# A window-attention block on one NeuronCore: x2 evicted by ScalarE, other orders on all queues, and groups handed to the second convolution from SBUF to SBUF

## The reference

```python
x = x + _conv_bn(x, dw0_w, dw0_s, dw0_b, groups=C)       # 3x3 depthwise
x = x + _ffn(x, f0_w1, f0_s1, f0_b1, f0_w2, f0_s2, f0_b2) # 64 -> 128 -> relu -> 64
x = x + _windowed_attn(x, wq, wkv, pos, scale_p, dwc_w, dwc_b, proj_w, proj_b)
x = x + _conv_bn(x, dw1_w, dw1_s, dw1_b, groups=C)
x = x + _ffn(x, f1_w1, f1_s1, f1_b1, f1_w2, f1_s2, f1_b2)
```

## Time and profile before

| | us |
|---|---|
| median of 3 runs (194.59 to 196.1) | 194.67 |
| the profiled execution, its own time | 195.5 |
| its span, first to last instruction | 193.7 |

### The profile page before, as it was taken

One profiled execution on the slowest core, in us unless ns is written; L12 is line 12 of the kernel. 1 busy time (PEld: TensorE's weight loads), 2 busy tenths in 40 slices (PEclk: granted clock), 3 DMA queues, 4 the chain that ended last, 5 costly groups with the idle time before them and its releaser, 6 DMA issues.

```text
span 193.7 us, 6645 instructions
## 1 busy us (share of the span) xinstructions
PE 164.9 (85%) x2840; PEld 79.9 (41%) x2840; DVE 109.2 (56%) x269; ACT 78.7 (41%) x144; POOL 67.7 (35%) x99
## 2 busy tenths in 40 slices
PE   7977989369929959989999476999997999995994
PEld 3322432334514525736636255358343434321141
DVE  1185269924664668769869869679254256002044
ACT  2052558224334326365480450672351615441122
POOL 3000207035145152254375384392046336330000
PEclk9999999856997999999999997899999999997599
DMA  5999998500000000000005306217017174757813
GB/s 150 284 292 229 208 216 167 141 3 0 3 2 3 0 3 3 3 3 5 3 3 157 58 3 170 43 58 154 8 61 175 63 167 130 174 170 187 210 54 108
DMA packets 18028, 18.77 MB, mean 97 GB/s; under 512 B 1104, under 2 KB 17744, under 8 KB 17872
## 3 DMA queue, kind: packets, MB, share of 16 engines
q1 hardware_dynamic: 17568, 17.83, 38.6%
q10 hardware_dynamic: 432, 0.52, 1.1%
HBM read 14.16 MB, written 4.19 MB: 95 GB/s over the span
## 4 chain that ended last, share of the span: by engine, by line
PE 37%; issue 13%; DVE 11%; POOL 9%; ACT 5%; DMA 4%; SPq 1%; DVEq 0%; POOLq 0%; ACTq 0%
PE ps L623 9%; PE ps L703 4%; PE ps L649 3%; PE ps L643 3%; PE ps L688 3%; POOL y L372 3%; DMA mid<-x 2%; DMA xc<-mid 2%; PE ps L824 2%; POOL x L382 2%; PE ps L815 2%; PE ps L727 2%; DVE k L997 2%; PE ps L763 2%; POOL k L349 2%
## 5 line engine op out<-in xcount | busy, mean ns | idle before, releaser
L623 PE MATMUL ps<-xc,dwf 96*32 96x480 f32 (+3 forms) x408 | 45.4, 582 | 2.2 <-DMA xc<-mid 2.1
L623 PEld LDWEIGHTS ps<-xc,dwf 96*32 96x32 f32 x408 | 11.9, 113 | 31.2 <-issue 25.9
L366 POOL TENSOR_TENSOR qt<-q 128x512 f32<-128x512 f32 x8 | 10.2, 1273 | 36.9 <-ACT q L461 36.9
L431 ACT ACTIVATE hid<-ps,wts 128x512 f32<-128x512 f32 x28 | 17.7, 681 | 6.5 <-PE ps L643 6.5
L349 POOL TENSOR_TENSOR k<-k 128x640 f32<-128x640 f32 x8 | 12.3, 1538 | 22.4 <-ACT k L449 22.4
L643 PE MATMUL ps<-x,w1s 64*128 64x512 f32 x60 | 17.9, 675 | 2.3 <-ACT x L424 1.6
L424 ACT ACTIVATE x<-ps,wts 128x512 f32<-128x512 f32 x15 | 10.2, 682 | 21.2 <-PE ps L623 21.2
L649 PE MATMUL ps<-hid,w2s 128*64 128x512 f32 x60 | 17.9, 642 | 0.2 <-ACT hid L431 0.2
L688 PE MATMUL ps<-x,wts 64*64 64x512 f32 x32 | 10.2, 712 | 8.0 <-DVE kvm L1043 5.6
L1068 DVE TENSOR_SCALAR x<-ps,bsum 128x512 f32<-128x512 f32 x7 | 5.2, 749 | 19.8 <-PE ps L649 19.8
L461 ACT ACTIVATE q<-q 128x512 f32<-128x512 f32 x8 | 5.0, 630 | 25.9 <-DVE q L1004 25.8
(11 more groups left out here) (133 smaller groups left out, 279.0 us busy)
## 6 DMA issues: line engine op xcount, KB each, us to landing
xc<-in_x SPq DMA_DIRECT2D x16, 240.0 KB, 10.3
xc<-mid SPq DMA_DIRECT2D x16, 240.0 KB, 4.3
xc<-in_x SPq DMA_DIRECT2D x8, 256.0 KB, 9.9
mid<-x SPq DMA_DIRECT2D x8, 256.0 KB, 2.1
xc<-mid SPq DMA_DIRECT2D x8, 256.0 KB, 3.4
out<-x SPq DMA_DIRECT2D x7, 256.0 KB, 4.5
tab<-in_tables SPq DMA_DIRECT2D x1, 1024.0 KB, 11.8
wts<-in_weights SPq DMA_DIRECT2D x1, 644.0 KB, 7.8
```

What stands on the lines that cost most here:

```text
L366: eng.tensor_tensor(qt[:, g % QB, 0:GC], q2[:, g % 2, 0:GC], q1[:, :], ALU.mult).then_inc(qt_ready, 1)
L431: eng.activation(hid[:, m % 2, a, :], bank(P_H + a), ACT.Relu, bias=ww(f"fb1_{m // NG}")).then_inc(h_ready[a], 1)
L623: last = eng.matmul(out_ps[32 * q:32 * q + 32, :, :, to], dwf[:, s, q % 2, i, :], src[:, :, :, of], start=(i == 0), stop=False, skip_group ...
```

## The change

x2 of the first eight groups is evicted by ACT, in four instructions, not by DVE; DVE keeps the second kind. The four stand behind `root` on ACT's queue. `take_v_rest` no longer waits for `k_rest`; `k_rest` waits for `take_v_rest`. The sums over the padding move from step 2 to set-up and step 1, and the query of group 1 waits for them. `key_value_full` stands behind `ffn1` in steps 3 and 4, and the query there waits for the eviction of the step before. `take_kv_rest` moves behind `k_guard` from step 5 on. `q_guard` goes from POOL to ACT, as a second square root in `root`. POOL does `third` ahead of `y_sum` and `v_masks` behind it. At the end of PE's list `attend(7)` stands ahead of `conv(11)`, and `turn_y(6)` ahead of `ffn1(11)`. `mid` is gone: each group goes from `x3` to `xc` by 12 DMAs, four blocks of 32 partitions for each of three shifts. The stores of groups 2 to 7's output all stand behind the last of these on SP. `third(c)` waits until the DMAs of group c - 2 have landed.

```diff
...
-                b, g = m % NB, m % NG
+                b, g = m % NB, m
...
+            def rows_on_chip(c):
+
+                b = c % NB
+                for dy in (1, 0, 2):
+                    to = slice(max(0, 1 - dy) * HW, PX - max(0, dy - 1) * HW)
+                    of = slice(max(0, dy - 1) * HW, PX - max(0, 1 - dy) * HW)
+                    for k in range(4):
+                        src = x3[32 * k:32 * k + 32, c % 2, :].rearrange("p (j n) -> p j n", j=GP)
+                        eng.dma_start(xc[32 * dy:32 * dy + 32, b, k:8:4, to], src[:, :, of]).then_inc(xc_in[b], 16)
...
             for c in range(NG):
-                if c >= 4:
+                if 4 <= c < 6:
                     eng.wait_ge(x2_ready, NG + c - 3)
-                    eng.dma_start(by_channel(out)[c - 4], x2[:, c - 4].rearrange("p j n -> p (j n)")[:, 0:GC].rearrange("p (j n) -> p j n", j=GP)).then_inc(stored, 16)
+                    eng.dma_start(by_channel(out)[c - 4], flat(x2[:, c - 4]).rearrange("p (j n) -> p j n", j=GP)).then_inc(stored, 16)
                 eng.wait_ge(x3_ready, c + 1)
-                eng.dma_start(by_channel(mid)[c], x3[:, c % 2, :].rearrange("p (j n) -> p j n", j=GP)).then_inc(mid_out, 16)
-                eng.wait_ge(mid_out, 16 * (c + 1))
                 eng.wait_ge(conv_ps, NG + c - NB + 1)
-                rows(mid, NG + c)
-            for c in range(NG - 4, NG):
+                rows_on_chip(c)
...
-            def q_guard(g):
-                eng.wait_ge(foc_ready, g + 2)
-                eng.tensor_scalar(geps[:, g, :], foc[:, g + 1, 1, :], EPS, None, ALU.mult).then_inc(geps_ready, 1)
...
             def third(c):
                 eng.wait_ge(xw_ready, c + 1)
                 if c >= 2:
-                    eng.wait_ge(mid_out, 16 * (c - 1))
+                    eng.wait_ge(xc_in[(c - 2) % NB], 96 + 192 * ((c - 2) // NB + 1))
...
-            for n in range(13):
+            for n in range(12):
                 if 0 <= n - 4 < NG:
                     add_pads(n - 4)
                 if 0 <= n - 2 < NG:
                     cube_k(n - 2)
                 if 1 <= n < 5:
                     cube_q(n - 1)
-                if n >= 11:
-                    y_sum(n - 6)
                 if 0 <= n - 7 < NG:
                     third(n - 7)
+                if n >= 6:
+                    y_sum(n - 6)
                 if 0 <= n - 2 < NG:
                     v_masks(n - 2)
-                if 6 <= n < 11:
-                    y_sum(n - 6)
-                if 0 <= n - 3 < NG:
-                    q_guard(n - 3)
                 if 5 <= n <= NG:
                     cube_q(n - 1)
-            y_sum(NG - 1)
-            third(NG - 2)
-            third(NG - 1)
+            y_sum(6)
+            y_sum(7)
+            third(5)
+            third(6)
+            third(7)
...
             def take_v_rest(g):
-                eng.wait_ge(krest_ready, g + 1)
+                eng.wait_ge(rest_ps, g + 1)
+                if g >= 1:
+                    eng.wait_ge(qn_ps, g)
+                if g >= 2:
+                    eng.wait_ge(kvr_ps, g - 1)
...
             def root(f):
                 eng.wait_ge(ratio_ready, f + 1)
-                eng.activation(foc[:, f].rearrange("p k s -> p (k s)"), rat[:, 1, :], ACT.Sqrt).then_inc(foc_ready, 1)
+                if f < NG:
+                    eng.activation(foc[:, f], rat[:, 1, 0:10], ACT.Sqrt).then_inc(foc_ready, 1)
+                if f >= 1:
+                    eng.activation(geps[:, f - 1], rat[:, 1, 10:20], ACT.Sqrt, scale=EPS * EPS).then_inc(geps_ready, 1)
+
+            def second(m):
+                eng.wait_ge(f_ps, m + 1)
+                if m == 0:
+                    eng.wait_ge(bsum_ready, 1)
+                src, by = bank(m % 2), bsum[:, 0:1]
+                for j in range(GP):
+                    eng.activation(x2[:, m, j, 0:WIN].rearrange("p (x h w) -> p x h w", x=2, w=WR), squares_of(src, j),
+                                   ACT.Identity, bias=by)
+                eng.activation(x2[:, m, :, WIN:WIN + 32].rearrange("p j (h w) -> p j h w", w=2), right_of(src), ACT.Identity, bias=by)
+                eng.activation(x2[:, m, :, WIN + 32:WIN + 64].rearrange("p j (w h) -> p j w h", h=2), bottom_of(src, HW),
+                               ACT.Identity, bias=by).then_inc(x2_ready, 1)
...
-            for n in range(1, 13):
+            second(0)
+            eng.wait_ge(pad_ratio, 1)
+            eng.activation(kpn[:, 2:3], kpn[:, 3:4], ACT.Sqrt).then_inc(pad_root, 1)
+            for n in range(1, 5):
+                if n >= 2:
+                    q_sixth(n - 2)
+                    k_square(n - 2)
+                q_square(n - 1)
+                take_v_full(n - 1)
+                hidden(n)
+                if n >= 2:
+                    k_sixth(n - 2)
+                first(n + 1)
+                if n >= 2:
+                    root(n - 2)
+                second(n)
+                if n >= 2:
+                    take_q_norms(n - 2)
+                take_v_rest(n - 1)
+            for n in range(5, 12):
...
+                if n - 2 < NG:
+                    q_sixth(n - 2)
+                if n - 2 < NG + 1:
+                    root(n - 2)
+                if m is not None and m < NG:
+                    second(m)
+                if n == 9:
...
-            take_yt(NG - 1)
+            first(11)
+            take_projected(5)
+            take_yt(6)
+            hidden(11)
+            take_projected(6)
+            take_yt(7)
             first(12)
-            take_projected(NG - 1)
+            take_projected(7)
...
                 if g == 0:
                     eng.wait_ge(set_up, 1)
                     eng.wait_ge(ecol_ready, 1)
-                if 0 <= n - 3 < NG:
+                if g == 1:
+                    eng.wait_ge(ones_set, 1)
+                if g >= 1:
+                    eng.wait_ge(q_ready, g)
+                if n >= 5:
                     eng.wait_ge(kvx_ready, n - 2)
-                elif g >= 1:
-                    eng.wait_ge(q_ready, g)
+                elif n >= 4:
+                    eng.wait_ge(kvx_ready, n - 3)
...
             def key_value_full(g, n):
                 eng.wait_ge(kf_ready, g + 1)
                 eng.wait_ge(v_ready, g + 1)
-                if g == 0:
-                    eng.wait_ge(ones_set, 1)
                 if n - 2 < NG:
-                    eng.wait_ge(q_ready, n - 1)
+                    eng.wait_ge(q_ready, n if n < 5 else n - 1)
...
             for n in range(1, 5):
-                if n >= 3:
-                    key_value_full(n - 3, n)
                 query(n - 1, n)
                 kv_full(n - 1, n)
                 ffn1(n, n)
+                if n >= 3:
+                    key_value_full(n - 3, n)
                 conv(n + 1, n + 1)
                 ffn2(n)
...
-                if n == 2:
+                if n == 1:
                     setup_pads()
...
-                if 6 <= n < 11:
+                if n >= 6:
                     turn_y(n - 6, n)
                 if n - 1 < NG:
                     kv_full(n - 1, n)
+            conv(10, 11)
+            attend(6, 11)
+            project(4, 11)
+            ffn1(10, 11)
+            turn_y(5, 11)
+            ffn2(10)
+            attend(7, 12)
             conv(11, 12)
-            attend(7, 12)
             project(5, 12)
+            turn_y(6, 12)
             ffn1(11, 12)
-            turn_y(6, 12)
+            project(6, 13)
             ffn2(11)
-            project(6, 13)
             turn_y(7, 13)
...
             def k_rest(g):
-                eng.wait_ge(rest_ps, g + 1)
+                eng.wait_ge(vrest_ready, g + 1)
                 if g >= 1:
-                    eng.wait_ge(qn_ps, g)
                     eng.wait_ge(k_ready, g)
-                if g >= 2:
-                    eng.wait_ge(kvr_ps, g - 1)
...
             def second(m):
-                s, g = divmod(m, NG)
                 eng.wait_ge(f_ps, m + 1)
-                src, by = bank(m % 2), bsum[:, s:s + 1]
-                if s == 1:
-                    eng.tensor_scalar(x2[:, g].rearrange("p j n -> p (j n)")[:, 0:GC], src, by, None, ALU.add).then_inc(x2_ready, 1)
-                    return
-                for j in range(GP):
-                    eng.tensor_scalar(x2[:, g, j, 0:WIN].rearrange("p (x h w) -> p x h w", x=2, w=WR), squares_of(src, j),
-                                      by, None, ALU.add)
-                eng.tensor_scalar(x2[:, g, :, WIN:WIN + 32].rearrange("p j (h w) -> p j h w", w=2), right_of(src), by, None, ALU.add)
-                eng.tensor_scalar(x2[:, g, :, WIN + 32:WIN + 64].rearrange("p j (w h) -> p j w h", h=2), bottom_of(src, HW),
-                                  by, None, ALU.add).then_inc(x2_ready, 1)
+                eng.tensor_scalar(flat(x2[:, m % NG]), bank(m % 2), bsum[:, 1:2], None, ALU.add).then_inc(x2_ready, 1)
...
-            second(0)
+
```

(104 more changed lines are left out.)

70 lines of the change are left out of this document (29 added, 41 removed).

## The result

The changed kernel takes 190.2 us (median of 4 runs, 189.6 to 194.6), the kernel before beside it 195.2 us (194.6 to 196.1): a ratio of 0.973 (95% interval 0.967 to 0.979). It is faster, by a third of what was predicted (179.1 us), and outside the range. The profiled execution took 190.28 us with a span of 188.5, that is 5.2 us less span than before, where 15.6 less were forecast.

What follows compares the result with a forecast made beforehand. PE, busy 164.9 of 193.7 us, was taken as the limit, by its own list or by what it waits for. The stage terms summed to -18.6 us, plus 3 for collisions -15.6, giving 179.1 us, range 172 to 188.

Steps and rivals of the forecast that it cites:

- The last convolutions: conv12 to conv15: 19.54 to 16.2 us, -3.3; SP's 36 issues at 0.451 us set the end.
- collisions: DVE with POOL at new places: 3 us added to the sum, 0.97 each in about three of ten steps.
- Rival 2: Last three groups: SP's issues decide; near 1.007 us each they take 20 us more, 199 us; chance 0.10.
- After conv15: The stretch after convolution 15: nothing changes, 193.7 - 185.
- Query 1: Start to query of group 1: 26.92 to 28.1 us, +1.1, as it now waits for the padding sums.
- rival 1: Early steps stay slow: low clock after query 1's wait, x2 on ACT holding queries 2 and 3; 185.5 us; chance 0.17.
- x2 on ACT: x2's four instructions on ACT, before query 1 and in the early steps: taken as 0.8 us, bounds 0.7 and 2.7.
- chain from query 1 to 2: Query 1 to query 2: 14.86 to 8.1 us, -6.7; the pads' 4 us go and a chain of operations remains.
- Rival 3: Steps 2 to 4: a collision on ratios delays root, x2 and the next query by 1 us each; 182 us; chance 0.10.
- Steps 6 to 9: 54.75 to 50.3 us, -4.4: norm6-to-norm6 loop falls from 13.31 to 11.6; PE waits 4.0 in step 8.
- Steps 10 to 12: 29.51 to 32.8 us, +3.3: new waiting at turn_y(5), as POOL has third ahead of y_sum.
- Steps 3 to 5: Query 2 to 3: 15.40 to 9.3 us; query 3 to step 5: 10.16 to 9.3; step 5: 13.86 to 12.3.

Runs made afterwards that it cites:

- the first experiment: The changed kernel with 52 extra DMAs in SP's idle time, in seven forms between SBUF and DRAM places, to price an issue; 189.3 us (one run).

## Why the prediction was wrong in size, point by point

- **The last convolutions** were the step that failed, and in it the price of an issue. The sum was 36 x 0.451 + 2.0 - 2; measured are 24.18 us for the issues, 1.46 from the end of the last to conv15, and a start 2.38 ahead of conv12: 23.26. The landing and the start were right to half a microsecond, the price was 0.67 instead of 0.451. It was taken from the median of the earlier trace rows, loads from DRAM, because nothing tied an issue's time to its bytes. That was true (256 KB cost what 64 KB cost), but the rows held no DMA between two places in SBUF, and the first experiment shows that this is what counts. Of the 10.4 us that the sum missed in the span, this is 7. The other step that failed is the low clock behind PE's waits, which the sum put at nothing or took off: it cost 1.7 us at query 1, 1.6 in steps 6 to 9, some 1.4 behind turn_y(5) and 1.7 in conv15, 6.4 in all. The 3 us that the forecast had set aside for collisions made up for a part of it, which is luck and not foresight.
- **Rival 2** so had the right mechanism and a price that was too high for it: at 0.67 the issues take the whole gain of this stage and 3.7 us more, but not the 15.6 of all stages. The rule on joining small transfers ("DMA: Bandwidth & Descriptors", "Rules for kernel authors", in the Trainium skill) pointed the right way. But what the runs show is a price per issue: a DMA of 256 KB within SBUF paid 0.608.
- **After conv15** nothing was to change. Conv15 itself ran at the lower level behind a wait of 3.87 us, 1.7 us of the 1.8. The forecast had seen this for conv14 of the kernel before (the row at 177.12 in the earlier trace rows) and counted it as removed.
- **Query 1** came when it should (28.24 against 28.1) after 2.33 us of waiting (2 were named), and the first half of rival 1 came with it: query and kv_full ran at the low level and took 3.56 us instead of 1.88, 1.7 more. Its second half did not: x2 on ACT was there in time for queries 2 and 3. (Two sums of the forecast are 0.1 off: 28.1 less 26.92 is 1.2, and its chain from query 1 to 2 adds up to 8.0.)
- **x2 on ACT** took 1.1 us, bounded by 0.7 and 2.7, taken as 0.8. Rival 3, where it would have held the next query, didn't happen.
- **Steps 6 to 9.** The loop from norm6 to norm6 is 12.97 and 12.81 us, not 11.6. On DVE:

```profile
87.56 0.82 DVE L1044 TENSOR_REDUCE nrm<-k 128x10 f32<-128x640 f32 x1 [1.17 <-ACT k L459]
...
95.25 1.87 DVE L1025 TENSOR_TENSOR k<-kraw,ewide 128x640 f32<-128x640 f32 x1
...
100.53 0.82 DVE L1044 TENSOR_REDUCE nrm<-k 128x10 f32<-128x640 f32 x1 [1.17 <-ACT k L459]
...
113.34 0.82 DVE L1044 TENSOR_REDUCE nrm<-k 128x10 f32<-128x640 f32 x1 [1.17 <-ACT k L459]
```

k_guard (L1025) takes 1.87 us here and 0.82 in steps 1 to 4, and POOL's rows show what it coincides with:

```profile
95.16 1.27 POOL L368 TENSOR_TENSOR qt<-q 128x512 f32<-128x512 f32 x1 [3.72 <-ACT q L465]
```

cube_q starts 0.1 us before it (and so again 12.8 us later), and k_guard ends 0.7 us after cube_q has; so it does in the two other groups where they overlap (1.43 and 1.37 us). No run moved cube_q. k_guard's extra 1.05 us is most of the 1.3; POOL's add_pads, which waits for take_kv_rest and now runs just ahead of cube_k (0.27 us), is most of the rest. The collisions that the forecast expected were right in kind and fall here, not all of them on the path: k_guard over its eight groups takes 9.8 us instead of 6.6. The Trainium skill ("GPSIMD Engine Reference", "Specifications") has POOL share its way to SBUF with DVE instructions of two SBUF inputs, which k_guard is; the trace agrees, as norm6, with one, takes 0.82 at 100.53 while POOL is at third. On PE the stage shows the wait that was forecast (52.10 less 48.03 is 4.07 us, forecast 4.0), but a clock of 0.97 as before: the 1.6 us of low clock, which the forecast had taken off, stayed. Its "about 2 more of window_conv" are 4.3 in the trace before (1.16 twice and 2.00), by which the same working gives 50.9.
- **Steps 10 to 12.** The wait at turn_y(5) was forecast at 3.3 us and is 3.17; what was not counted is the low clock behind it (1.57 us for 0.90 at L768, 1.67 for 1.08 at L674).
- **Steps 3 to 5** were right to a quarter of a microsecond, or better than forecast in step 5. There a window_conv (L850, 2.06 us at 58.50) now stands ahead of ffn1, where PE had waited before; the list of changes does not name this. The reason given first, that the padding sums and key_value_full leave the path, holds without x2 on ACT, but for the 2.1 us above.

## What to carry to other kernels

Price a DMA issue by a row of the same kind (which memories stand at its two ends), and where the trace has none, let the range follow what the count of issues multiplies: 36 times a price that is off by 0.22 us is 7.9 us, more than the 5.0 that the change gained. A hand-over that saves a round trip but takes three times the issues (12 for 4) is worth it only where its queue has time; look at how many groups come to the queue at once. An engine that waits for work can take a share of the issues.
